# One output-projection tile at the head of TensorE's work in every mixer step, with y kept unsplit and split per tile

## What is computed

```
def _L0_attn_ref(hidden_states, in_proj_w, conv_w, conv_b, dt_bias, D, norm_w, out_proj_w):
    ...
    proj = hidden_states @ in_proj_w.T
    gate, xBC, dt = jnp.split(proj, [INTER, INTER + CONV_DIM], axis=-1)
    ...
    xBC = jax.nn.silu(jnp.swapaxes(conv, 1, 2))
    ...
    yg = y * jax.nn.silu(gate)
    yg_g = yg.reshape(Bsz, S, NG, GROUP)
    rstd = jax.lax.rsqrt(jnp.mean(jnp.square(yg_g), axis=-1, keepdims=True) + EPS)
    out = (yg_g * rstd).reshape(Bsz, S, INTER) * norm_w
    return out @ out_proj_w.T
```

## Time and profile before

| | us |
|---|---|
| median of 3 runs | 1699.41 |
| lowest and highest | 1698.5, 1699.82 |
| the profiled execution's own time | 1699.76 |
| its span, first to last instruction | 1698.0 |
| PE busy in the span | 1594.4 |
| DVE busy | 1307.5 |
| POOL busy | 1074.4 |
| ACT busy | 1040.7 |

### The profile page before, as it was taken

How to read it: one execution, slowest core, us unless ns; L and a number is a source line. 1 busy time by engine, 2 the same in 40 slices (tenths; PEclk the granted TensorE clock), 3 DMA queues, 4 the chain that set the end, 5 groups by cost and what they waited for, 6 DMA issues and landing times. The chain is left out here.

```text
span 1698.0 us, 26982 instructions
## 1 busy us (share of the span) xinstructions
PE 1594.4 (94%) x8296; PEld 1229.0 (72%) x8296; DVE 1307.5 (77%) x1705; ACT 1040.7 (61%) x2144; POOL 1074.4 (63%) x790
## 2 busy tenths in 40 slices
PE   7979999999999999989999999989999999999989
PEld 4757767767677777767687777767677776767667
DVE  6679588885979678895879668895879768894975
ACT  4457575675747665675747665675747666575731
POOL 2029685695829775595928776495938777395921
PEclk9899999999999999999999999999999999999999
DMA  3033222221213222231213222231313212131111
GB/s 113 1 106 106 88 68 72 90 90 57 88 69 106 69 76 81 76 106 57 87 45 112 87 75 81 65 105 57 100 45 112 87 63 94 51 112 62 57 38 50
DMA packets 73679, 131.92 MB, mean 78 GB/s; under 512 B 10944, under 2 KB 10944, under 8 KB 73280
## 3 DMA queue, kind: packets, MB, share of 16 engines
q1 hardware_dynamic: 73536, 130.09, 23.4%
HBM read 127.44 MB, written 2.62 MB: 77 GB/s over the span
## 5 line engine op out<-in xcount | busy, mean ns | idle before, releaser
L161 PE MATMUL bank<-h_hi,mx_w_hi 128*128 128x512 f32 x1152 | 481.9, 418 | 4.3 <-DVE mx_acc L887 2.3
L162 PE MATMUL bank<-h_lo,mx_w_hi 128*128 128x512 f32 x1152 | 456.2, 396 | 0.0
L163 PE MATMUL bank<-h_hi,mx_w_lo 128*128 128x512 f32 x1152 | 456.2, 396 | 0.0
L834 POOL TENSOR_TENSOR mx_w_lo<-mx_w_raw,mx_w_hi 128x512 fp32r<-128x512 f32 x144 | 321.4, 2233 | 209.5 <-ACT mx_w_hi L829 208.5
L887 DVE SCALAR_TENSOR_TENSOR mx_acc<-bank,mx_cw,mx_acc 128x510 f32<-128x510 f32 (+2 forms) x480 | 356.2, 742 | 105.5 <-ACT mx_acc L872 96.1
L1229 DVE TENSOR_TENSOR mx_mix<-mx_mix,mx_cbt 128x1536 f32<-128x1536 f32 x128 | 325.4, 2542 | 0.8
L1007 POOL TENSOR_TENSOR mx_y<-mx_y,mx_sg 128x512 f32<-128x512 f32 x128 | 249.7, 1951 | 57.9 <-DVE mx_y L1248 55.2
L161 PEld LDWEIGHTS bank<-h_hi,mx_w_hi 128*128 128x128 f32 x1152 | 220.6, 191 | 63.4 <-issue 18.6
L1078 ACT ACTIVATE mx_mix<-mx_csb,mx_gncs 128x256 f32<-128x256 f32 x512 | 218.2, 497 | 64.0 <-POOL mx_csb L994 29.8
L163 PEld LDWEIGHTS bank<-h_hi,mx_w_lo 128*128 128x128 f32 x1152 | 220.0, 191 | 50.3
L162 PEld LDWEIGHTS bank<-h_lo,mx_w_hi 128*128 128x128 f32 x1152 | 221.0, 192 | 38.9
(11 more groups left out here) (162 smaller groups left out, 2236.3 us busy)
## 6 DMA issues: line engine op xcount, KB each, us to landing
mx_csb<-cs_rows SPq DMA_DIRECT2D x128, 512.0 KB, 3.9
mx_w_raw<-in_w_in SPq DMA_DIRECT2D x144, 256.0 KB, 3.7
mx_wo_raw<-in_w_out SPq DMA_DIRECT2D x64, 256.0 KB, 3.2
res<-in_x SPq DMA_DIRECT2D x8, 256.0 KB, 4.4
f_base_raw<-in_base_wt SPq DMA_DIRECT2D x2, 1024.0 KB, 6.3
out<-res SPq DMA_DIRECT2D x8, 256.0 KB, 2.0
...
```

The source lines that it names most:

```text
L161: nc.tensor.matmul(out, w_hi, x_hi, start=first, stop=False)
L162: nc.tensor.matmul(out, w_hi, x_lo, start=False, stop=False)
L163: return nc.tensor.matmul(out, w_lo, x_hi, start=False, stop=last)
L834: self.nc.gpsimd.tensor_tensor(self.w_lo[:, w % 3, :, :], self.w_raw[:, w % 3, :, :], self.w_hi[:, w % 3, :, :].bitcast(F32), ALU.subtract ...
```

## The change

`yg_hi` and `yg_lo` go. `y` has a slot for each of the 16 steps and is kept unsplit. A tile p (0 to 15) belongs to step p: tiles 8 to 15 are the first quad of the same group, tiles 0 to 7 the second quad of the group before. PE runs tile p at the head of step p (`project_out`). One step earlier ACT rounds the tile's piece of y (`round_tile`, into one of two slots `yt_hi`), and POOL makes the remainder (`split_tile`). ACT copies out the tiles of the first quad, one a step (`keep_first_quad`); DVE adds those of the second quad and adds the group to `res` at the end of steps 1 to 8 (`add_quads(g, st - 1)`, `add_group(g, st - 1)`), behind `silu_gate` and, in odd steps, `split_wo`. Between the groups no tile is left. Group 0 has no tiles in its first 8 steps, and 8 tiles follow the last group. The loop over groups now turns between step 8 and step 9 (`loop_halves`). The matmuls are the same in number and size.

```diff
         wo_raw = sb("wo_raw", [P, 2, HID])
-        wo_hi = sb("wo_hi", [P, QUAD, HID], F32R)
-        wo_lo = sb("wo_lo", [P, QUAD, HID], F32R)
+        wo_hi = sb("wo_hi", [P, XT, HID], F32R)
+        wo_lo = sb("wo_lo", [P, XT, HID], F32R)
+        yt_hi = sb("yt_hi", [P, 2, QUAD, P], F32R)
+        yt_lo = sb("yt_lo", [P, 2, QUAD, P], F32R)
...
-        y = sb("y", [P, 2, HALF])
+        y = sb("y", [P, STEPS, HALF])
...
+        def loop_halves(eng, steps, tail):
+
+            half = XT + 1
+            steps(0, range(half), True)
+            with eng.Fori(0, NG - 1) as g:
+                steps(g, range(half, STEPS), True)
+                tail(g, True)
+                steps(g + 1, range(half), True)
+            steps(NG - 1, range(half, STEPS), False)
+            tail(NG - 1, False)
+
+        def tile_of_step(p):
+
+            q = 1 if p < XT else 0
+            return q, p % XT // 4, p % 4
+
+        def has_tile(g, p):
+            return p >= XT or not first(g)
...
+                nc.gpsimd.tensor_tensor(y[:, st, :], y[:, st, :], sg[:, st % 2, :], ALU.mult).then_inc(s["yg"], 1)
+
+            def split_tile(g, p):
+                q, hf, t = tile_of_step(p)
+                pool.wait_ge(s["yhi"], 1 + STEPS * g + p + 1)
+                nc.gpsimd.tensor_tensor(yt_lo[:, p % 2, :, :], y_tile(q, hf, t), yt_hi[:, p % 2, :, :].bitcast(F32),
                                         ALU.subtract).then_inc(s["ylo"], 1)
...
-                    if st >= 1:
-                        split_y(g, st - 1)
+                    if st + 1 < STEPS:
+                        if has_tile(g, st + 1):
+                            split_tile(g, st + 1)
+                    elif st == STEPS:
+                        split_tile(g + 1, 0)
                     if st >= 3:
                         sum_squares(g, st - 1)
...
                 group(g, g + 1 < NG)
+            for p in range(1, XT):
+                split_tile(NG, p)
...
+            def round_tile(g, p):
+                q, hf, t = tile_of_step(p)
+                act.wait_ge(s["yg"], 1 + STEPS * g + (XT - 1 + hf if q == 0 else hf - 1))
+                act.wait_ge(s["out"], 1 + STEPS * g + p - 1)
+                nc.scalar.activation(yt_hi[:, p % 2, :, :], y_tile(q, hf, t), ACT.Copy).then_inc(s["yhi"], 1)
...
+            def keep_first_quad(g, p):
+
+                n = p - XT
+                act.wait_ge(s["out"], 1 + STEPS * g + p + 1)
+                act.wait_ge(s["outsb"], 1 + TT * g + n + 1)
+                nc.scalar.activation(m.gacc[:, n, :], O_BANK[p % 2][:, :], ACT.Copy).then_inc(s["gcopy"], 1)
...
+                    if st > XT:
+                        keep_first_quad(g, st - 1)
+                    if here or more:
+                        evacuate(gn, un)
                     if st >= 1:
...
                         square(g, st - 1)
...
+                    if here and has_tile(g, st + 1):
+                        round_tile(g, st + 1)
+                    if here or more:
+                        decay_from_second(gn, stn)
                     tanh_gate(g, st)
                     if here or more:
                         tanh_conv(gn, un)
-                round_y(g, STEPS - 1)
-                square(g, STEPS - 1)
...
+                    if st % 2 == 0:
+                        split_wo(g, st // 2)
+
+            def tail(g, more):
+                keep_first_quad(g, STEPS - 1)
+                round_tile(g + 1, 0)
...
                 if more:
                     evacuate(g + 1, 1)
+                    square(g, STEPS - 1)
                     ip.round_w(act, g + 1, 2)
-                root(g, 0)
-                if more:
                     tanh_conv(g + 1, 1)
                     evacuate(g + 1, 2)
                     tanh_conv(g + 1, 2)
                     evacuate(g + 1, 3)
-                root(g, 1)
-                if not more:
+                    tanh_conv(g + 1, 3)
+                    ip.round_w(act, g + 1, 3)
+                    evacuate(g + 1, 4)
+                    tanh_conv(g + 1, 4)
+                    root(g)
+                else:
+                    square(g, STEPS - 1)
+                    round_tile(NG, 1)
+                    root(g)
+                    for p in range(2, 6):
+                        round_tile(NG, p)
                     next_ln.root(act, 0)
...
                 dve.wait_ge(s["y"], 1 + STEPS * g + st + 1)
-                dve.wait_ge(s["sq"], 1 + STEPS * g + max(st - 1, 0))
-                dve.wait_ge(s["ylo"], 1 + STEPS * g + max(st - 1, 0))
+                dve.wait_ge(s["ylo"], 1 + STEPS * g + (XT if st >= XT else 0))
...
             def add_quads(g, n):
 
-                dve.wait_ge(s["gcopy"], 1 + 8 * g + 8)
-                dve.wait_ge(s["out"], 1 + OUTS * g + 8 + n + 1)
+                dve.wait_ge(s["gcopy"], 1 + TT * (g - 1) + n + 1)
+                dve.wait_ge(s["out"], 1 + STEPS * g + n + 1)
                 nc.vector.tensor_tensor(m.gacc[:, n, :], O_BANK[n % 2][:, :], m.gacc[:, n, :],
                                         ALU.add).then_inc(s["gsum"], 1)
 
             def add_group(g, n):
 
-                dve.wait_ge(s["gsum"], 1 + 8 * g + n + 1)
-                nc.vector.scalar_tensor_tensor(m.res[:, n, :], m.gacc[:, n, :], rms[:, n // 4, n % 4:n % 4 + 1],
+                dve.wait_ge(s["inv"], 1 + g)
...
-                        ip.tap(dve, gn, un, 1)
-                    if here or more:
-                        ip.tap(dve, gn, un, 2)
-                    if st in (2, 4, 6):
-                        split_wo(g, st // 2 - 1)
-                    elif st == 7:
-                        split_wo(g, 3)
-                    elif st in (11, 13, 15):
-                        split_wo(g, (st - 3) // 2)
-                    if here or more:
-                        ip.tap(dve, gn, un, 3)
+                        ip.taps(dve, gn, un)
                     silu_gate(g, st)
+                    if st % 2 == 1:
+                        split_wo(g, st // 2)
+                    if 1 <= st <= XT and has_tile(g, st - 1):
+                        add_quads(g, st - 1)
+                        add_group(g, st - 1)
                     if st == STEPS - 2 and more:
...
-                split_wo(g, 7)
+
+            def tail(g, more):
                 skip_y(g, STEPS - 1)
                 if more:
                     silu_conv(g + 1, 0)
                     head_constants(g + 1)
-                mean_square(g, 0)
-                if more:
...
-                if more:
                     taps(g + 1, 2)
+                    silu_conv(g + 1, 2)
+                    taps(g + 1, 3)
                     keep_bc(g + 1, 0)
-                    silu_conv(g + 1, 2)
-                mean_square(g, 1)
-                if not more:
-
+                    mean_square(g)
+                    silu_conv(g + 1, 3)
+                    taps(g + 1, 4)
+                    keep_bc(g + 1, 1)
+                    inverse(g)
+                else:
+                    add_quads(NG, 0)
+                    add_quads(NG, 1)
+                    mean_square(g)
+                    inverse(g)
+                    add_group(NG, 0)
+                    add_group(NG, 1)
+                    for n in (2, 3):
+                        add_quads(NG, n)
+                        add_group(NG, n)
...
-            def project_out(g, q, hf, tiles=range(4)):
-
-                pe.wait_ge(s["ylo"], 1 + STEPS * g + 8 * q + 7 + hf)
-                pe.wait_ge(s["wolo"], 1 + XT * g + QUAD * (q + 1))
-                for t in tiles:
-                    n = 8 * q + 4 * hf + t
-                    if n < 2:
-                        pe.wait_ge(s["cbt"], 1 + 2 * g + 2)
-                    elif n < 10:
-                        pe.wait_ge(s["gcopy"], 1 + 8 * g + n - 1)
-                    else:
-                        pe.wait_ge(s["gsum"], 1 + 8 * g + n - 9)
-                    for r in range(QUAD):
-                        at = slice(t * P, (t + 1) * P)
-                        last = three_pass(nc, O_BANK[n % 2][:, :], m.yg_hi[:, r, hf, at], m.yg_lo[:, r, hf, at],
-                                          wo_hi[:, r, :], wo_lo[:, r, :], r == 0, r == QUAD - 1)
-                    last.then_inc(s["out"], 1)
+            def project_out(g, p):
+
+                q = tile_of_step(p)[0]
+                i, bank = p % 2, O_BANK[p % 2]
+                pe.wait_ge(s["ylo"], 1 + STEPS * g + p + 1)
+                pe.wait_ge(s["wolo"], 1 + XT * g + (QUAD if q == 0 else 0))
+                if p > XT + 1:
+                    pe.wait_ge(s["gcopy"], 1 + TT * g + p - XT - 1)
+                elif p >= 2:
+                    pe.wait_ge(s["gsum"], 1 + TT * g + p - 1)
+                elif isinstance(g, int) and g == NG:
+                    pe.wait_ge(s["gcopy"], 1 + TT * g - 1 + p)
+                else:
+                    pe.wait_ge(s["cbt"], 1 + 2 * g + 2)
+                for r in range(QUAD):
```

(36 more changed lines are left out.)

178 lines of the change are left out of this document (65 added, 113 removed).

## The result

| | before | changed |
|---|---|---|
| median | 1699.62 us (4 runs, 1698.5 to 1700.26) | 1726.95 us (4 runs, 1723.88 to 1732.71) |
| ratio, 95% interval | 1 | 1.0165 (1.0136 to 1.0195) |
| profiled execution: time, span, mean clock | 1699.76, 1698.0, 0.984 | 1732.71, 1730.9, 0.979 |

The change costs 27.3 us where 11.5 were forecast. The profiled execution of the changed kernel is the slowest of its four, 5.8 us above the median, so sums made from its trace come to 32.9 us of span and not to 27.

A forecast was written before the change was run, and what follows sets the result against it. PE was taken to bound the kernel. Six groups +5.4, group 0 -24.6, last group +19.6, behind it +7.4 and clock +3.4 gave +11: span 1709, time 1711 us, 0.7% slower; range 1694 to 1730.

The forecast's parts named there:

- six groups, 181.5 + 9.4 + 3.2 = 194.1: Middle groups: wait-free PE time, plus head waits, plus chain between groups, against 193.2 us each before: +5.4 us in all.
- What it takes away: Waits of PE's transposes for x go, steps 9 to 15 take 10.38 us: 11.7 us a group back.
- The waits at the heads: Heads of steps 2 to 9: PE waits for add_quads, 0.62 us after even, 1.74 after odd steps; 9.4 a group.
- The chain between the groups: Between groups, without tiles, PE waits on alternating ACT and DVE work for silu and B and C: 3.2 us, bounds 0 to 5.
- The ends: Group 0 and the tiles behind the last group: some extra waits, last tile ending at m + 36.5 (m: last mixing's start).
- Group 0: First group, without tiles in its first 8 steps: 168.6 us against 193.2 before, -24.6.
- The last group up to its last mixing: Last group's steps to its final mixing: 15 x 10.38 + 9.4 = 165.1 us against 145.48 before, +19.6.
- Half clock: PE running at half rate after waits: two falls put between the groups, +3.4 us.
- (a): Rival: additions don't hold PE up, 1645 us; weaker form, short split_wo and closed chain, 1679; together 0.15.
- (b): Rival: the terms cancel to within 3.4 us of no change; chance 0.13.
- (c): Rival: DVE itself bounds odd steps, reaching silu_gate later than m + 0.74 (m: mixing start); +28, 1739 us; chance 0.10.
- (d): Rival: each odd head wait brings PE's clock down for a 3.41 us stretch; 48 us added, 1759 us; chance 0.05.

The follow-up runs named there:

- e9: The changed kernel with the loop over groups written out on PE alone, DVE and ACT still looping: 1711.28 us, ratio 1.0063 to the kernel before.
- e5: The changed kernel with DVE's add_quads and add_group moved ahead of split_wo, nothing else: 1718.56 us, ratio 1.0110 to the kernel before.
- e4: The changed kernel with add_quads and add_group of steps 1 to 8 moved on DVE to between decay product and scale_x: 1681.51 us, ratio 0.9875.
- e3: The changed kernel with PE's loop turn alone moved behind the in-projection of step 9: 1715.93 us, ratio 1.0081 to the kernel before.

## Why the prediction was wrong in size

The direction held, the cause it named was real, and the time lies in the range, though by luck: none of the terms that the range was made of is the one that failed. The size is wrong by the sum's line "six groups, 181.5 + 9.4 + 3.2 = 194.1". **The failed step**: the working there has PE's work, the heads and the chain between groups, and nothing for the turn of the loop, though the change moves the turn from behind a block of output matmuls to a place with only mixing ahead of it. It costs 4.1 us a group, 24.8 in all: 19.0 of idle "issue" time (23.1 less some 4.05 in two gaps before the groups, which e9 has too), and six stretches at half rate that cost some 1.6 us each, less the 0.56 that this head waits anyway. e9 is the test: without PE's turn the ratio is 1.0063, that is +10.7 us, against +11.5 forecast. In part that agreement is luck: smaller misses cancel (below), and e9 still has DVE's and ACT's turns and the later heads.

Point by point, on the profiled execution, whose 1730.9 us of span stand against 1709 forecast:

- **What it takes away**: right. Steps 10 to 15 take 10.33 us flat (forecast 10.38), and no transpose in them waits. Rounding and splitting y inside a step holds nobody up: POOL's remainder shows in three waits, at the ends.
- **The waits at the heads**: right in number and size. 50 waits for `gacc`, and six more that the turn swallows; 0.56 and 1.63 as the profile prints them, in turn, and by the starts 2.08 and 3.15 us from mixing to the tile, against 2.07 and 3.19. `split_wo` as it now stands:

```profile
L1295 DVE SCALAR_TENSOR_TENSOR mx_wo_lo<-mx_wo_raw,mx_nw,mx_wo_hi x64: 744/1148/1160, 126.5 to 1636.8; 128x512 fp32r<-128x512 f32 x64
```

  At most 1.16 us, where I had taken 1.20 between bounds of 0.74 and 1.49. The first odd head of a group waits only 1.22, since the split of step 1 takes 0.75. The rule of the Trainium skill (SBUF — State Buffer, "SBUF: two separate sides") that I cited fits: here the split meets POOL's masks, and in e5 it takes 0.74 behind them.
- **The chain between the groups**: 3.2 forecast, 1.30 and 1.88 printed, at the two places named. (The range counts this term six times, 19 us, though it stands in seven groups, 22 us.)

```profile
668.92 0.69 PE L1438 MATMUL bank<-mx_acc 128*128 128x256 f32 x2 [1.30 <-DVE mx_acc L1249]
...
672.36 0.50 PE L159 MATMUL bank<-mx_wo_hi,mx_yt_hi 128*128 128x512 f32 x1 [1.88 <-DVE mx_cbt L1256]
```

- **The ends**: mixed. The first mixing starts at 117.49, not 120.32: -2.8, not forecast. Group 0: -1.0 against the forecast. The last group up to its last mixing: -3.8, since I charged its last step with a projection that isn't there (it takes 7.61 us, not 10.38), and the heads came a little short. Behind it: +7.8. The last tile ends at 1679.73, m + 44.3 where 36.5 was forecast:

```profile
1635.43 0.65 PE L1476 MATMUL bank<-mx_mix,mx_xd 128*64 128x256 f32 x4
...
1640.81 0.50 PE L159 MATMUL bank<-mx_wo_hi,mx_yt_hi 128*128 128x512 f32 x1 [3.85 <-POOL mx_yt_lo L1043]
...
1652.54 0.79 PE L159 MATMUL bank<-mx_wo_hi,mx_yt_hi 128*128 128x512 f32 x1 [2.68 <-POOL mx_yt_lo L1043]
...
1668.36 1.82 PE L139 MATMUL bank<-ident,mx_csb 128*128 128x128 f32 x8 [1.88 <-ACT mx_csb L131]
1670.95 0.80 PE L159 MATMUL bank<-mx_wo_hi,mx_yt_hi 128*128 128x512 f32 x1 [0.76 <-POOL mx_yt_lo L1043]
```

```profile
1635.43:1679.73 44.30, 35.13 (x145) 27.43 (x144) 22.57 (x41) 12.98 (x23) 13.46 (x10) 0.81 0.00 0
```

  The waits for tiles 0 and 2 came as forecast. The 1.88 us for the normalised input did not stand in my bookkeeping, nor that PE would run this stretch at PEclk 0.81: its 145 matmuls take 35.1 us, and 28.1 before.
- **Half clock**: I put two falls and 3.4 us. There are six behind the turns, two between groups, and three among the tiles behind the last group.
- In sum: 24.5 in the six groups (24.8 for the turns), -2.8, -1.0, -3.8, +7.8, +0.4 behind the last tile, 0.2 of rounding, and -3.4 for the clock, which is now inside the other lines: 21.9, from 1709 to 1730.9.

**The rivals.** (a) is dead as a forecast and true as an edit: e4 is the kernel in which the additions hold nobody up. It gave 49 us of the 66 that I had put on it; most of the rest is the wait of 1.2 us at step 8, and the head of step 9, where the turn's gap stays. (b) is dead: the time is 27 us from before. (c) is dead: `silu_gate` starts at m + 0.74 and m + 0.73 in the steps shown. (d) is dead in its place: behind none of the 28 odd waits of 1.2 or 1.6 us does PEclk fall. Its mechanism came true elsewhere: it fell behind all six gaps of 2.8 to 4.1 us, and behind two of the seven of 1.88. The warning of the Trainium skill (TensorE: Matmul & The Clock Gate, "HAM oscillation — how this bites in real kernels") fits the gap of the turn, which comes back in every group with its fall, and not these heads, where the trace shows none.

**Left open**: PE's gap at the turn goes with the time that its instruction packet takes, but why that is 1.2 us in one group and 2.8 in another is not shown, nor what stands between the packet's end and PE's start. That long queued matmuls hide a turn, or most of it, is shown by the time of e3 and by the trace of the kernel before; how far PE's sequencer must be ahead for it was not tried.
